# Selective scan laid out as 4 states x 32 channels, with half of the products with C on GpSimd

## The reference

```python
x = x + 0.5 * L0_ffn(norm(x));  x = x + L0_attn(norm(x));  x = x + 0.5 * L0_ffn(norm(x))
x = x + 0.5 * L1_ffn(norm(x));  x = x + L1_attn(norm(x));  x = x + 0.5 * L1_ffn(norm(x))
```

```python
u = silu(conv(x @ W_in.T));  dlt, B, C = split(u @ W_x.T)
delta = softplus(dlt @ W_dt.T + b_dt)
dA[t,d,n] = exp(delta[t,d] * A[d,n]);  dBu[t,d,n] = delta[t,d] * B[t,n] * u[t,d]
h[t,d,n] = dA[t,d,n] * h[t-1,d,n] + dBu[t,d,n]       # h restarts every 32 positions
y[t,d] = sum_n h[t,d,n] * C[t,n];  out = (y * silu(res)) @ W_out.T + b_out
```

## Time and profile before

| | us |
|---|---|
| median of 3 runs (lowest, highest) | 1054.3 (1046.04, 1056.78) |
| profiled execution | 1056.04 |
| its span, first to last instruction | 1054.3 |
| busy: PE, DVE, ACT, POOL | 911.8, 768.3, 655.8, 516.0 |
| TensorE's mean granted clock | 0.937 |

### The profile page before, as it was taken

How to read it: one execution, slowest core, us unless ns; L and a number is a source line. 1 busy time by engine, 2 the same in 40 slices (tenths; PEclk the granted TensorE clock), 3 DMA queues, 4 the chain that set the end, 5 groups by cost and what they waited for, 6 DMA issues and landing times.

```text
span 1054.3 us, 11228 instructions
## 1 busy us (share of the span) xinstructions
PE 911.8 (86%) x3358; PEld 431.3 (41%) x3358; DVE 768.3 (73%) x1717; ACT 655.8 (62%) x1030; POOL 516.0 (49%) x412
## 2 busy tenths in 40 slices
PE   6557877888889888999999999999999889978975
PEld 5334334343444344445354444435443343333432
DVE  3222514988599769995999688978998989799821
ACT  4435558568757866677778765897687437634221
POOL 2112135555647464645565555666475545555311
PEclk9668898999899989999999999999999898998976
DMA  3000106523553446336337545545354717665320
GB/s 144 10 0 25 67 0 217 196 100 124 197 190 111 137 175 227 116 130 213 136 122 233 186 154 171 190 168 198 128 185 171 236 47 254 222 190 184 107 90 11
DMA packets 49325, 151.83 MB, mean 144 GB/s; under 512 B 4976, under 2 KB 13296, under 8 KB 49264
## 3 DMA queue, kind: packets, MB, share of 16 engines
q1 hardware_dynamic: 49264, 151.12, 41.9%
HBM read 148.21 MB, written 2.88 MB: 143 GB/s over the span
## 4 chain that ended last, share of the span: by engine, by line
PE 47%; DVE 26%; ACT 12%; issue 6%; POOL 5%; DMA 2%; SPq 0%; DVEq 0%; POOLq 0%; ACTq 0%
PE yp L1484 10%; DVE dA L983 10%; PE mp L1428 4%; PE mp L1443 4%; PE fp L1249 4%; PE pp L1363 4%; PE pp L1229 3%; PE fp L1265 3%; ACT L117 3%; DVE hs L990 3%; DVE he L941 2%; PE mp L1229 2%; PE pp L1333 2%; ACT dA L1208 2%; PE mp L1452 2%
## 5 line engine op out<-in xcount | busy, mean ns | idle before, releaser
L710 POOL TENSOR_TENSOR dbu<-du,b_row 128x1024 f32<-128x1024 f32 x128 | 301.5, 2359 | 169.7 <-DVE dA L983 151.0
L983 DVE TENSOR_TENSOR_SCAN dA<-dA,dbu 128x512 f32<-128x512 f32 x256 | 312.4, 1220 | 67.5 <-POOL dbu L710 34.9
L1484 PE MATMUL yp<-hs,ident 128*128 128x512 f32 x512 | 268.4, 628 | 14.1 <-DVE hs L990 13.9
L1208 ACT ACTIVATE dA<-delta,pr 128x512 f32<-128x512 f32 x256 | 173.6, 685 | 80.5 <-DVE hs L990 76.3
L990 DVE TENSOR_TENSOR hs<-dA,c_row 128x512 f32<-128x512 f32 x256 | 176.9, 691 | 9.8 <-PE yp L1484 1.1
L117 ACT ACT_TABLE_LOAD x130 | 166.8, 1283 | 2.4
L1484 PEld LDWEIGHTS yp<-hs,ident 128*128 128x128 f32 x512 | 89.2, 195 | 142.6 <-issue 84.8
L1428 PE MATMUL mp<-cont,ex_ 64*128 64x512 f32 x128 | 79.1, 701 | 12.7 <-DVE he L941 11.4
L1265 PE MATMUL fp<-w,hT 128*128 128x129 f32 x512 | 68.6, 285 | 13.7 <-ACT hT L1044 7.0
L1432 PE MATMUL mp<-cont,ex_ 64*128 64x512 f32 x128 | 79.3, 703 | 0.1
L1265 PEld LDWEIGHTS fp<-w,hT 128*128 128x128 f32 x512 | 64.2, 197 | 36.4 <-ACT hT L1044 14.9
(11 more groups left out here) (216 smaller groups left out, 1353.8 us busy)
## 6 DMA issues: line engine op xcount, KB each, us to landing
b_row<-held SPq DMA_DIRECT2D x104, 512.0 KB, 4.9
c_row<-held SPq DMA_DIRECT2D x104, 512.0 KB, 4.3
gsp<-gheld SPq DMA_DIRECT2D x64, 512.0 KB, 6.2
xin<-L_attn_x SPq DMA_DIRECT2D x8, 256.0 KB, 4.7
out<-xb SPq DMA_DIRECT2D x8, 256.0 KB, 3.4
ex_<-c_ex SPq DMA_DIRECT2D x1, 1001.0 KB, 6.8
b_row<-c_ps SPq DMA_DIRECT2D x1, 768.0 KB, 8.2
pr<-c_pr SPq DMA_DIRECT2D x1, 567.0 KB, 9.1
```

Source lines behind the costliest of these rows:

```text
L710: pool.tensor_tensor(out=dbu[:, j % 2, :].rearrange("p (r t) -> p r t", r=2), in0=d, in1=b_n, op=ALU.mult).then_inc(dbu_r.sem, 1)
L983: dve.tensor_tensor_scan(out=dA[:, half], data0=dA[:, half], data1=dbu[:, j % 2, half], initial=0.0, op0=ALU.mult, op1=ALU.add).then_inc(h ...
L1208: act.activation(out=dA[:, r * SEQ:(r + 1) * SEQ], in_=delta[:, i % 2, c, :], func=ACT.Exp, scale=mA[:, c, 2 * k + r:2 * k + r + 1]).then_ ...
L1484: pe.matmul(yp[:, :], lhsT=ident[:, :], rhs=hs[:, j % 2, r * SEQ:(r + 1) * SEQ], start=(s % PAIRS == 0 and r == 0), stop=(s % PAIRS == PAI ...
```

## The change

The scan's tiling is turned. A partition now holds one of 4 blocks of 4 states and one of 32 channels ("lane"); 256 channels are 8 groups of 32. A step is a chunk c, a state k of each block, and a pair of groups j: 2 x 4 x 2 = 16 steps a sequence as before, each with two halves of 512 columns. What follows from it:

- `rows` replaces `spread`: two times four transfers of 256 KB a sequence bring B and C for all states (bc4). In their place thread U (`deltas`) writes du and delta of each chunk to HBM and reads each back four times, once per block, into u4 and d4. Those and bc4 are single; du and delta are no longer doubled. The exponential and dbu read d4 and u4.
- du and its starting positions are formed by chunk instead of at once.
- Steps with an odd number (`on_pool`): the scan writes hs instead of dA, and POOL multiplies hs by C in place, by half. Even steps stay on DVE.
- PE waits for both products of a step and adds each half into 32 partitions of yp, with a weight `stack` of 128x32 that sums the four blocks; a part of yp takes 4 matmuls a chunk, all four parts 16 as before.
- A is also held in the new layout. The order strings are new: ACT's has its delta parts of the next sequence after 20, 16, 11, 11, 10, 18 and 27 of the running sequence's 32 exponentials (after all 32 before).

The core of the diff:

```diff
+OWN = STATES // BLOCKS
+LANES = P // BLOCKS
+GROUPS = INNER // LANES
+PER = GROUPS // IC
+STEPS = IC * OWN * PER // 2
+STEP_ORDER = [(c, k, j) for c in range(IC) for k in range(OWN) for j in range(PER // 2)]
...
+                        for s in range(BLOCKS):
+                            sp.dma_start(bc4[block_rows(s), h, :, :, :].rearrange("p w k t -> p (w k t)"),
+                                         held[i % 2, h, s:s + 1, :].broadcast_to([LANES, 4 * SEQ])
+                                         ).then_inc(bc_in[h].sem, 16)
...
+                        sp.dma_start(uheld[i % 2, c, :, :], du[:, c, :]).then_inc(u_out[c].sem, 16)
...
+                        for s in range(BLOCKS):
+                            sp.dma_start(u4[block_rows(s), own, :], by_lane(uheld)).then_inc(u_in[c].sem, 16)
...
+            def c_thread():
...
+                            pool.wait_ge(hs_r.sem, 2 * n + r + 1)
+                            pool.tensor_tensor(out=hs[:, n % 2, half], in0=hs[:, n % 2, half],
+                                               in1=bc4[:, k // 2, 1, k % 2, :], op=ALU.mult).then_inc(hc_p, 1)
...
+                            if on_pool(n):
+                                if r == 0 and n >= 2:
+                                    dve.wait_ge(sum_ps.sem, 2 * (n - 1))
+                                dve.tensor_tensor_scan(out=hs[:, n % 2, half], data0=dA[:, half],
+                                                       data1=dbu[:, n % 2, half], initial=0.0, op0=ALU.mult,
+                                                       op1=ALU.add).then_inc(hs_r.sem, 1)
+                                continue
...
+                            if h >= 2 and on_pool(h // 2 - 1):
+                                act.wait_ge(hs_r.sem, h - 1)
+                            elif h >= 2:
+                                products.wait(act, h - 2)
+                            act.activation(out=dA[:, r * SEQ:(r + 1) * SEQ], in_=d4[:, g, :], func=ACT.Exp,
+                                           scale=mA[:, IC + g, k:k + 1]).then_inc(dA_r.sem, 1)
...
-                            pe.matmul(yp[:, :], lhsT=ident[:, :], rhs=hs[:, j % 2, r * SEQ:(r + 1) * SEQ],
-                                      start=(s % PAIRS == 0 and r == 0), stop=(s % PAIRS == PAIRS - 1 and r == 1)
+                        products.wait(pe, 2 * n + 1)
...
+                            pe.matmul(yp[LANES * g:LANES * (g + 1), :], lhsT=stack[:, :],
+                                      rhs=hs[:, n % 2, r * SEQ:(r + 1) * SEQ], start=(k == 0), stop=(k == OWN - 1)
                                       ).then_inc(sum_ps.sem, 1)
```

More of the change, by code:

```diff
@@ new lines, in rows @@
+                    for h in range(2):
+                        yield True
+                        if h == 0:
+                            sp.wait_ge(bc_out.sem, bc_out.at(i, 16))
+                        if i >= 1:
+                            sp.wait_ge(dbu_r.sem, dbu_r.at(i - 1, last_of_half(h)))
+                            done = (i - 1) * STEPS + last_of_half(h)
+                            products.wait(sp, 2 * max(n for n in range(done) if on_pool(n)) + 1)
+                            products.wait(sp, 2 * max(n for n in range(done) if not on_pool(n)) + 1)
+                        for s in range(BLOCKS):
+                            sp.dma_start(bc4[block_rows(s), h, :, :, :].rearrange("p w k t -> p (w k t)"),
+                                         held[i % 2, h, s:s + 1, :].broadcast_to([LANES, 4 * SEQ])
+                                         ).then_inc(bc_in[h].sem, 16)
@@ L643, in p_thread @@
                 half(b_enc).then_inc(ro_half, 1)
+                step(pool.memset(stack[:, :], 0.0))
+                for s in range(BLOCKS):
+                    ins = pool.affine_select(out=stack[:, :], in_=stack[:, :], compare_op=ALU.not_equal, fill=1.0,
+                                             base=-LANES * s, pattern=[[-1, LANES]], channel_multiplier=1)
+                    if s < BLOCKS - 1:
+                        step(ins)
+                ins.then_inc(consts, 1)
                 for kind, n in P_TURNS:
@@ new lines, in s_thread @@
+                        pool.tensor_tensor(out=dbu[:, n % 2, :].rearrange("p (r t) -> p r t", r=2),
+                                           in0=u4[:, c * PER + 2 * j:c * PER + 2 * j + 2, :],
+                                           in1=b_n.broadcast_to([P, 2, SEQ]), op=ALU.mult).then_inc(dbu_r.sem, 1)
+            def c_thread():
+                for i in range(BATCH):
+                    for s, (c, k, j) in enumerate(STEP_ORDER):
+                        n = i * STEPS + s
+                        if not on_pool(n):
+                            continue
+                        for r in range(2):
+                            half = slice(r * SEQ, (r + 1) * SEQ)
+                            yield True
+                            pool.wait_ge(hs_r.sem, 2 * n + r + 1)
+                            pool.tensor_tensor(out=hs[:, n % 2, half], in0=hs[:, n % 2, half],
+                                               in1=bc4[:, k // 2, 1, k % 2, :], op=ALU.mult).then_inc(hc_p, 1)
```

316 lines of the change are left out of this document (164 added, 152 removed).

## The result

The changed kernel is slower, by 1 to 2.5%: 1069.8 us as the median and in the profiled execution, 1.018 times the kernel before (95% interval 1.010 to 1.025). I had forecast 980 us, and 935 to 1052 as the range. The span is 1068.0 us instead of 1054.3, at a mean granted clock of 0.887 instead of 0.937.

A forecast was written before the change was run, and what follows sets the result against it. The busiest engine, PE then DVE, was taken as the bound: leaders' 666.2 us at occupancy 0.905 give 736, so 1054.3 - 81 + 8 = 981 us, stated as 980. Forecast range 950 to 1020; wider range 935 to 1052.

The forecast's parts named there:

- What bounds the kernel: Scanned part: busiest engine sets the pace, PE in seven stretches, DVE in the eighth; 761.3 of 817.4 us, occupancy 0.931.
- The sum: Scanned part after the change: leaders' work 666.2 us at occupancy 0.905 (bounds 0.88 to 0.931) gives 736 us.
- The clock: PE's granted clock in the scanned part: 0.92 to 0.97 expected at some 81% busy.
- The change of weight shape: PE entering and leaving the 128x32 sums: 0.13 us charged on each side, 33 us in all.
- The wait for both products: PE before a step's first sum: work behind it waits at most 1.18 us more, priced within the occupancy's bounds.
- Every second product to POOL: Products with C: DVE loses 88.4 us; POOL gains 128 products at 1.18 us (1.09 to 1.27), 151 us.
- Transfers: Delta and du through HBM: data 8 to 13 us after du, 8 us charged at first start, later starts covered.
- my 70%: POOL rival's threshold: kernel slower than before once more than about 191 of POOL's 275 us of waits remain.
- that rival's sum: POOL becomes the bound: 618 us work plus 275 us waits, stretches 893, kernel 1138 us; chance 0.12.
- its rival: HBM round trip not hidden: 8 to 13 us at seven starts, kernel 1058 us, no change; chance 0.06.
- The two matmuls do overlap: Rival on PE's sums claimed they do not overlap: PE keeps 683.1 us, kernel 1052, no change; chance 0.04.
- Partly spoilt: Rival: POOL's queue brings the scanned part's occupancy to 0.82 to 0.86, kernel 1020 to 1043 us; chance 0.08.

The follow-up runs named there:

- old, sums at once: Kernel before, with TensorE waiting for both halves of a step's product, then adding both with the same 128x128 weight: 1087.6 us, ratio 1.030.
- sums into 64 rows: Changed kernel with a 128x64, half-zero weight, so a step's two sum matmuls run one after the other: 1104.9 us, ratio 1.048.
- changed kernel with filler: Changed kernel with four added zero-weight 128-column matmuls on PE before three of four steps wait for their products: 1105.4 us, ratio 1.049.
- old, quarter sums at once: Kernel before, with a step's sum as two 128x32 matmuls issued together after both halves of the product: 1072.6 us, ratio 1.018.

## Why the prediction was wrong, step by step

**What bounds the kernel: the step that failed.** I took the busiest engine of each stretch for its bound and divided its work by an occupancy. The two runs with sums at once in the old kernel speak against it: between them a tenth of PE's work left a stretch that PE filled to 93%, and the stretch got 3.4% shorter; over the whole scanned part 65 us less work on PE gave 15. The wait for both halves speaks against it from the other side: 32 us more with the same work. What these runs point to in its place is the way of a sequence's parts through four queues in a written order. A busy leader shows that the order kept it fed; it does not show that others waited only for it. That the chain of waits gave PE 47% was no better evidence, for a matmul in the chain may have started late because of what stood ahead of it in PE's queue. The Trainium skill, "Perfetto Trace Analysis", Identifying the Most-Contended Engine, advises to optimize the engine of highest occupancy first, and warns that matmul busy time is no good measure of how near TensorE is to its limit. This case bears out the warning, as the two stretches show; the advice it does not test, since the page does not go by matmul busy time.

**The sum.** In the prediction's own terms the leaders' work came out as 696.8 us (PE 627.7 in the first seven stretches, DVE 69.1 in the eighth) instead of 666.2, and the occupancy as 696.8/815.5 = 0.854 instead of 0.905, under the lower bound of 0.88. The 31 us of work are 34 us of time at 0.905, the occupancy the other 46.

**The clock.** I had 0.92 to 0.97 for the scanned part; it was 0.91, where the first seven stretches before had 0.98, and 0.82 to 0.88 in the four stretches in which PE is busy 71% to 82%. PE's other 2846 instructions, none of them changed, are busy 683 us before and 728 after, taken by themselves and counted once where they overlap one another. So the sums' group lost 128 us and PE 57: 45 came back as slower work, and for the other 27 us other matmuls had run beside the sums, so that PE stays busy without them:

| run | PE busy | sums | the others alone | clock |
|---|---|---|---|---|
| old, sums at once | 907.3 | 253.2 | 680 | 0.945 |
| before | 911.8 | 268.4 | 683 | 0.937 |
| sums into 64 rows | 931.3 | 241.4 | 703 | 0.916 |
| changed kernel with filler | 902.0 | 152.3 | 712 | 0.907 |
| old, quarter sums at once | 842.8 | 142.9 | 712 | 0.906 |
| old kernel, new orders | 957.6 | 267.1 | 715 | 0.900 |
| after | 855.1 | 140.0 | 728 | 0.887 |
| all products on DVE | 884.7 | 146.5 | 751 | 0.867 |

The lower the clock, the longer the same matmuls. PE idles 143 to 176 us of the span in the first three of these runs and 195 to 227 in the others. I had the clock as a reason for a lower occupancy, not as work that grows. What it costs in time no run isolates.

**The change of weight shape.** I charged 33 us for it. The busy time shows no such term: the old kernel in the new orders, whose sums keep the 128x128 weight, stands at 715 us, beside the quarter sums' 712 at nearly the same clock. Whether it adds idle time is not shown.

**The wait for both products.** I put it within the occupancy's bounds. In the old strings it costs 32 us, twice what the faster sums then give back. In the new ones it is free, so it does not account for this kernel's time, but it shows how large a wait without work can be.

**Every second product to POOL.** Right in kind (worth 32 us, in proportion to their number), and 1.271 us instead of 1.18, my upper bound, 10 us over 128. That is 1.84 times DVE's 0.691. The Trainium skill, "GPSIMD Engine Reference", Engine selection, says about twice for elementwise work with two inputs, and this trace comes near it.

**Transfers.** The first start was to lose 8 us to the trip. uheld was asked for at 177.22 and the exponential could start at 194.07, 17 us later:

```profile
177.22 0.42 SPq L528 DMA_DIRECT2D uheld<-du  x1
...
182.82 1.76 SPq L539 DMA_DIRECT2D u<-uheld  x4
...
184.62 1.85 SPq L545 DMA_DIRECT2D d<-dheld  x4
...
194.07 1.30 ACT L1278 ACTIVATE dA<-d,pr 128x512 f32<-128x512 f32 x2 [6.57 <-DMA d<-dheld]
194.79 1.23 DVE L1047 TENSOR_TENSOR_SCAN dA<-dA,dbu 128x512 f32<-128x512 f32 x1 [0.72 <-ACT dA L1278]
```

This is a timeline of SP, ACT and DVE (start, length, line, last the idle time and what ended it). SP writes delta after du and reads it in four parts behind the four of u, each group 1.8 us of issuing; I had priced one write and one group of reads. Yet that is not why the scan starts late, since it starts at 193.4 without any trip: I read ACT's string for the cover of delta and for table loads, and not DVE's, in which 28 F parts instead of 22 stand ahead of the first scan. Later starts were covered, as I said (ACT waits for d three times, 11 us in all), and the trip's 16 to 20 us lie in the stretches: without it the scanned part takes 801.4 us instead of 815.5.

**The rivals.** None came true as I had worked it out. POOL's waits for f_vv, fvar, dg and du, 275 us before, are still 201 us (65.9, 59.7, 60.9 and 14.7), over my 70%, and by that rival's sum the stretches need 618 + 201 = 819 us, near the 815.5 measured. The agreement is luck: the run without POOL's products has 156 us less work there and gains only 10 us, so POOL is not the bound, and the rule that I tied to those waits was wrong. The round trip costs 16 to 20 us, far less than the 77 of its rival. The two matmuls do overlap:

```profile
964.04 1.05 PE L1556 MATMUL yp<-hs,stack 128*32 128x512 f32 x4
```

Four instructions, a step's two halves, in 1.05 us. What I left out is a rival in which the work goes and the time stays. "Partly spoilt", 0.82 to 0.86, named the occupancy but gave it 0.08, for another cause, and its sum was off: 666 us at 0.82 make 812 and the kernel 1057, not 1043.

**What stays open.** What in the written order holds each layout is not settled. The trip accounts for the difference to the kernel before (without it the two are equal), but not for the 74 us that I had forecast as gain; the clock, the order and the waits of the layout can't be taken apart further with these runs, and that an order exists in which the new layout wins is neither shown nor excluded.

## What to carry to other kernels

Before a forecast divides work by occupancy, ask what the same stretch did when the leader had less to do; where four engines run a written order at 60 to 97%, work taken from one of them is worth a fraction (here a third, a quarter or nothing) and can cost time if it moves a wait. Read a change of layout and its new order as one thing: each part alone, in the old order, was slower or made no difference, and the old layout was 10% slower in the new one. And look at every engine's string for what now stands ahead of the first critical part.

## What the hardware showed that I had not expected

- The same 2846 matmul instructions were busy 683 us at a mean granted clock of 0.937, 728 at 0.887 and 751 at 0.867.
- On GpSimd du as one instruction of 1024 columns took 2.353 us, as two of 512 1.27 each: the half costs 8% more than half.
- Two reads queued one behind the other after their writes took 17 us from the first issue to the last landing, where a 256 KB write alone lands in 3.4 us.
